# Leaving out the constant products of the two routers in a two-layer token and mixture-of-experts kernel

## The reference

```
# layer 0 (rows normed; 8 experts, hidden size 288)
logits = x @ router_w + router_b;  probs = softmax(logits)
p, idx = top_k(probs, 2)
out   += sum over the two: p * (gelu(x @ w1[e] + b1[e]) @ w2[e] + b2[e])

# layer 1 (layernorm with gamma and beta; 8 experts, hidden size 768)
logits = x @ router_w;  probs = softmax(logits)
w, idx = top_k(probs, 2);  w = w / sum(w)
out   += sum over the two: w * (silu(x @ w1[e]) @ w2[e])
```

## Time and profile before

| | |
|---|---|
| median of 3 runs | 434.62 us (431.35, 434.62, 435.26) |
| the profiled execution | 431.57 us, of it 429.8 us span |
| TensorE, busy share and mean granted clock | 93%, 0.969 |
| weight loads / VectorE / ScalarE / GpSimd busy | 69% / 66% / 54% / 51% |
| all constant products (L1905) | 176, 46.9 us busy |
| of them in the two routers | 64 + 58 = 122 |

### The profile page before, as it was taken

How to read it: one execution, slowest core, us unless ns; L and a number is a source line. 1 busy time by engine, 2 the same in 40 slices (tenths; PEclk the granted TensorE clock), 3 DMA queues, 4 the chain that set the end, 5 groups by cost and what they waited for, 6 DMA issues and landing times.

```text
span 429.8 us, 11100 instructions
## 1 busy us (share of the span) xinstructions
PE 400.2 (93%) x3926; PEld 298.0 (69%) x3926; DVE 282.0 (66%) x1310; ACT 230.2 (54%) x424; POOL 219.3 (51%) x225
## 2 busy tenths in 40 slices
PE   8999989998889999998989889879999999999993
PEld 5653656666435666665545579438999999999993
DVE  6699999899884444445584368975565656555551
ACT  1387964541666666663353125574665656566550
POOL 5324789795046777765100003344566566566534
PEclk9999799999999999999699999969999999999998
DMA  8519200010222222231899970692243434243323
GB/s 243 109 46 240 60 0 2 2 37 2 88 93 66 82 78 75 80 80 47 251 252 249 235 190 1 121 151 75 44 58 55 65 48 66 46 66 54 47 21 35
DMA packets 38585, 38.29 MB, mean 89 GB/s; under 512 B 7331, under 2 KB 35793, under 8 KB 38517
## 3 DMA queue, kind: packets, MB, share of 16 engines
q1 hardware_dynamic: 27601, 22.84, 23.0%
q0 software_dynamic: 9024, 13.44, 16.3%
q10 hardware_dynamic: 1906, 1.30, 1.0%
HBM read 27.73 MB, written 10.53 MB: 89 GB/s over the span
## 4 chain that ended last, share of the span: by engine, by line
PE 28%; DMA 9%; DVE 9%; issue 3%; ACT 2%; POOL 1%; POOLq 1%; DVEq 0%; ACTq 0%
PE bank L2069 10%; PE bank L2114 9%; DMA out<-a,idx 8%; DVE h L1732 2%; PE bank L2357 1%; PE bank L1905 1%; DVE st L1245 1%; PE bank L2466 1%; POOL out L796 1%; PE bank L2039 1%; PE bank L2389 1%; PE bank L2363 1%; DMA a<-expert_rows 1%; PE bank L2438 1%; ACT reg L1049 1%
## 5 line engine op out<-in xcount | busy, mean ns | idle before, releaser
L796 POOL DMA_INDIRECT out<-a,idx x31 | 50.7, 1637 | 46.3 <-DMA out<-a,idx 36.3
L776 POOL DMA_INDIRECT reg<-xn_rows,idxs x59 | 57.6, 977 | 28.0 <-issue 14.3
L2069 PE MATMUL bank<-reg,xT 64*128 64x128 f32 x1116 | 69.2, 275 | 0.8 <-DVE reg L1647 0.8
L2069 PEld LDWEIGHTS bank<-reg,xT 64*128 64x128 f32 x1116 | 65.2, 188 | 0.9 <-DVE reg L1647 0.9
L2114 PE MATMUL bank<-reg 64*128 64x192 f32 x744 | 65.6, 323 | 0.0
L2114 PEld LDWEIGHTS bank<-reg 64*128 64x128 f32 x744 | 60.0, 187 | 0.0
L1081 ACT ACTIVATE reg<-reg 128x1152 f32 x31 | 36.1, 1163 | 33.8 <-PE bank L2114 33.8
L1676 DVE TENSOR_SCALAR a<-bank,gs 128x192 f32<-128x192 f32 x31 | 13.0, 418 | 53.4 <-PE bank L2114 53.4
L1905 PE MATMUL bank<-con 128*128 128x512 bf16 x176 | 46.9, 423 | 0.0
L784 POOL DMA_INDIRECT expert_rows<-a,idx x28 | 27.6, 987 | 14.6 <-DVE a L1673 8.5
L1905 PEld LDWEIGHTS bank<-con 128*128 128x128 bf16 x176 | 18.5, 109 | 22.8 <-issue 8.8
(11 more groups left out here) (370 smaller groups left out, 873.7 us busy)
## 6 DMA issues: line engine op xcount, KB each, us to landing
reg<-in_w2b SPq DMA_DIRECT2D x8, 576.0 KB, 10.9
reg<-in_w1b SPq DMA_DIRECT2D x8, 288.0 KB, 11.2
reg<-in_w1a SPq DMA_DIRECT2D x8, 216.0 KB
reg<-in_w2a SPq DMA_DIRECT2D x8, 216.0 KB
xn_rows<-xn SPq DMA_DIRECT2D x4, 384.0 KB, 2.8
reg<-in_w1b SPq DMA_DIRECT2D x8, 192.0 KB, 9.2
xn_rows<-xn SPq DMA_DIRECT2D x1, 1152.0 KB, 8.3
out<-h SPq DMA_DIRECT2D x1, 1152.0 KB
```

The lines of the kernel that those rows point to most:

```text
L776: pool.indirect_dma_start(xs[:, i % RING, 0:(D, D2)[l]], None, xd[l], bass.IndirectOffsetOnAxis(ap=idxs[:, i:i + 1], axis=0)).then_inc(xs_ ...
L796: pool.indirect_dma_start(out, bass.IndirectOffsetOnAxis(ap=idx2[:, i:i + 1], axis=0), ys[:, i % YRING, :], None, compute_op=ALU.add).then ...
L2069: ins = MM(bank[2 + 2 * p + a][:, c * P:(c + 1) * P], w1r[rs, p, col:col + hc], xT64[rs, p, k, :], start=(c == 0 and k == 0), stop=(c == n ...
```

## The change

`ranks(l)` no longer calls `keep_busy`. In both routers the three groups are gone, 122 products in all. The waits, the rank products, the one-hot products and their order stay as they are, and so do the other calls of `keep_busy`.

```diff
@@ def ranks(l):
-                keep_busy((24, 28)[l], 2)
                 pe.wait_ge(msk_ready, l + 1)
...
                 half = NAACT // 2
                 order = [*range(NAACT, NAP[l]), *range(half), *range(NAP[l], NA), *range(half, NAACT)]
-                keep_busy((16, 14)[l], 2)
                 pe.wait_ge(oneB_ready, l + 1)
                 for n, a in enumerate(order):
...
                 ins.then_inc(inv_mm, 1)
-                keep_busy((24, 16)[l], 7)
```

## The result

The changed kernel takes 444.28 us (median of 4 runs, 443.93 to 445.32) where the kernel before takes 434.51 us in the same comparison (431.35 to 435.26). The ratio is 1.0246, with a 95% interval of 1.0199 to 1.0293: slower by over 1%. The forecast was 437.2 us with a range up to 441.0, so the measured time lies outside it. Ratios here are of undisturbed runs, and a run more than 1.5% above the fastest of its kernel counts as disturbed; in e2, e12, e13 and e17 that spread may be the effect itself, so single times are given there.

What follows compares the result with a forecast made beforehand. Both expert stages were taken as bound by TensorE. Earlier starts (-1.3 us) and clock loss (+4.4) gave +3.1 us on the profiled execution; less 0.5 on average, +2.6 on the 434.62 us median gave 437.2 us, range 433.2 to 441.0.

Steps and rivals of the forecast that it cites:

- Bound and covers: Expert stages are bound by TensorE; removing both routers' first and second groups, which fill idle time, changes nothing.
- Earlier start: Without the third groups, experts start 0.6 us earlier in layer 0 and 0.7 in layer 1, together 1.3 us.
- The clock falls in both routers: Without the groups TensorE is almost idle in both routers, so both expert stages begin at 1.2 GHz.
- The clock comes back 2.5 to 5.3 us after dense work begins: At both expert starts; each stage loses 1.2 to 2.7 us, mean 2.2, together 4.4 us.
- The four places: Dense stretches from 49.40, 117.07, 206.79 and 285.07; the clock returned after 5.3, 2.5, 4.9 and 5.2 us.
- Rival B: Expert products raise the clock later than constant products did; 2.5 us per layer 0 tile, 4.2 in layer 1; chance 0.17.
- its larger case: One further tile at half clock in each layer, giving 443.9 us; outside the range.
- Rival C: The groups themselves delay the experts, router 0's third usually at half clock; median 433.3 to 435.2 us; chance 0.22.
- the prediction's 0.5 us: Average saving if router 0's third group runs at half clock in one execution in five, delaying experts about 2.5 us.

Runs made afterwards that it cites:

- e2: Changed kernel with the 16 constant products behind router 1's one-hot products put back; 444.1 us, ratio 1.0256 to the kernel before.
- e12: Changed kernel with 8 constant products behind router 0's one-hot products; single times from 433.2 to 449.0 us, in two groups.
- e13: Changed kernel with 5 unbroken pairs of constant fp32 96-row, 64-column products ahead of layer 0's experts; 434.03 us, ratio 0.9983, one run at 452.99.
- e17: Changed kernel with a constant imitation of two layer 0 tiles (transpositions, 96x64 pairs) ahead of the experts; 437.5, 442.1, 451.9 and 453.0 us.
- e3: Kernel before without its first and second groups in both routers, both third groups kept; 436.41 us, ratio 1.0097.
- e18: Changed kernel with two imitated layer 0 tiles ahead of the experts, single 128x128 products instead of 96x64 pairs; 435.9 to 437.9 us, ratio 1.0074.
- e5: Changed kernel with the ten transpositions of each layer 0 tile issued as ordinary products with the identity; one run, 464.61 us.
- e1: Changed kernel with the 24 constant products behind router 0's one-hot products put back; ratio 1.0102 to the kernel before; 435.72, 436.6, 437.68 us, one stray 974.
- e7: Kernel before without router 1's three groups (58 products), router 0's three kept; 437.14 us, ratio 1.0067.
- e10: Kernel before with router 0 cut to 12 constant products behind its one-hot products, router 1's three groups kept; 432.2 us, ratio 0.9952.
- e8: Changed kernel with 12 constant products behind router 0's one-hot products; 434.07 us, ratio 1.0025 to the kernel before.
- e4: Kernel before without router 0's third group (24 products), the other five groups kept; 441.0 us, ratio 1.0231.
- e16: Changed kernel with 5 unbroken single constant fp32 products of 128 rows by 128 columns ahead of layer 0's experts; 433.75 us, ratio 0.9981.

## Why the prediction was wrong, point by point

- **Bound and covers.** Right. Both expert stages are bound by TensorE: the +12.22 us of layer 0 arrive whole at the end. The first and second groups filled idle time only. What the prediction missed is their second value, which e3 shows: they let the third group run at full clock (5.34 us instead of 7.26).
- **Earlier start.** Right in kind; in layer 0 half in size, 0.30 us where 0.6 was forecast: `t_x(0)` did start at 129.12 (forecast 129.10) and `t_x(1)` at 130.41, but from there to the first product it took 0.38 us where the forecast left 0.1. In layer 1 it was 0.79 us where 0.7 was forecast, 0.5 of it because the gates' DMA was done sooner after the mask.
- **The clock falls in both routers.** Right (at 112.6, and 0.65 in the slice from 283).
- **The clock comes back 2.5 to 5.3 us after dense work begins.** This is the step that failed. In layer 1 it took 2.9 us and cost 1.33 us, inside the bounds. In layer 0 it took 26.2 us and cost 12.22 us where 2.2 were taken and 2.7 was the upper end. The sum of both layers, put at 4.4 us, measured 13.55. By tiles: at half clock one takes 4.74 us (from the g1 at 148.39 to that at 153.13), at full 2.52, and 26.2 x (1 - 2.52 / 4.74) = 12.3. The four places that the step rested on the earlier trace rows were all products on 128 rows. The step carried them over to pairs of products on 96 rows with a break in each tile, which the runs e13, e17 and e18 take apart in part. One of the four was also misread: TensorE was busy without a pause from 115.93, not from 117.07, so that return took 3.6 us and not 2.5.
- **Rival B was what happened**, with its mechanism, its layer and its consequence (443.9 us was its price for one late tile in each layer; 444.3 came, by five and a half tiles in one, so that the two times agree is chance). Its price for a tile, 2.5 us, measured 2.2 (4.74 less 2.52). It had 0.17, and the range left its larger case out. The earlier trace rows show the mixture only holding the level, and the prediction said so; no row bounded the return from above, and 5.3 us stood there as a bound all the same. The rule from the Trainium skill ("TensorE: Matmul & The Clock Gate", Part 4: PE-mode transpose), that a transposition doesn't count as array activity in the way a product does, pointed at layer 0, rightly. The one run of e5 does not bear out its reason here: with ordinary products in the same place the clock stayed at half for 32 us of the experts.
- **Rival C** has its grain: the third group at half clock does delay the experts, in e1 by 2.3 us (first product at 133.41 for 131.09). It is the smaller effect by far. Whether the kernel before has its third group at half clock in some executions, as the prediction's 0.5 us assumed, no trace shows. Its executions do differ in how long they stay at half clock: 435.78 us went with a mean clock of 0.961, 430.87 with 0.972.
- **Not settled:** why router 1's groups are worth 0.7% (e7; e10 against e8) when the profiled runs account for 0.5 to 1.6 us in its stretches; what exactly of a break and of a part-filled array keeps the clock down, rows or pairing; and why the same tiles lift the clock after 16 us in one run and after 31 in another.

## What to carry to other kernels

Before removing work that only keeps the array active, look at what runs behind it: how soon a stage at half clock recovers depends on its own products, and a stage bound by TensorE that fails to recover loses nearly half of that time. A trace that shows a stage holding the full clock does not show that it would reach it, so that return has no upper bound from such rows. If a constant group is needed, place it directly ahead of the stage, as long as the idle time there and no longer: 12 products did what 24, with two more groups ahead of them, did.

## What the runs showed of the hardware

- Levels were 1.00 and 0.50 only (slices of 1 us in between hold a change), and one and the same kernel lifted its clock or didn't from run to run: e12 433.2 to 449.0 us, e17 437.5 to 453.0.
- The level changed some time after TensorE had resumed or stopped: in the kernel before it fell at 116.1, 0.2 us after TensorE had resumed at 115.93, and in e12's profiled run it came back at 129.0, 0.8 us after the eighth constant product had ended.
- Layer 1's mixture (pairs of 64 rows by 128 columns, 6 transpositions among 66 products) lifted the clock in 2.9 us (the changed kernel) and layer 0's (pairs of 96 by 64, 10 among 30) in 16, 26 and 31 us (e4, the changed kernel, e17).
- Constant products without a break lifted it in all five kinds tried (e8, e13 to e16; 49 of 50 runs by their times); with the breaks of a layer 0 tile, the single 128x128 ones did in ten runs of ten and the 96x64 pairs failed in two or three of four.
